# A graph network with feed-forward layers on one core: the dense layers taken block by block through the first gather pass, and the target one-hots of seven slots made by one instruction

## The chip, the cores and the metric

The kernel runs on one core of one Trainium2 chip. The metric is the device time of one execution in microseconds (us). Before the change it is 5313.63 us, the median of three runs (5313.40 to 5313.65).

## The reference

x is 6250 rows of 256 floats. There are 206250 edges (src, dst), sorted by dst, each with a type of 500. Four layers follow each other, each added to x:

```
x = x + L0_gnn(layernorm(x))     # feat: t1 = feat@W1; per edge t1[src] + (feat[src]*feat[dst])@W2, scaled by degrees,
                                 # summed over dst; leaky_relu(0.01); each row divided by its norm
x = x + L0_ffn(layernorm(x))     # x @ weight.T + bias
x = x + L1_gnn(layernorm(x))     # per edge: linear(h[src]*rel[type]) * sigmoid gate, normed by degrees,
                                 # summed over dst; then linear(h + sum)
x = x + L1_ffn(layernorm(x))     # for the 3124 rows with the highest score x@wr: gelu MLP, times the score
```

What matters here: both graph layers need, for every node, the sum over its incoming edges of a row that belongs to the edge's source. The second graph layer reads rows that depend on the first graph layer and on the dense layer behind it, of every node.

## The kernel before

The nodes are 49 blocks (NB) of 128 rows. X holds x in SBUF. A block's edges are padded to 35 slots (C) of 128 edges, so there are 1715 slots (SLOTS); seven slots (SG) are a step, five steps (SPB) a block. The table of rows (256 values and one extra column, padded to 260) is stored in DRAM, t1_d for the first layer and t2_d for the second.

A pass goes over all slots. GpSimd (POOL) issues one indirect gather per slot (`gathers`, L574) into `gath`, a ring of 18 slots (RG); a slot is free again when TensorE (PE) has used it, which it tells every sixth slot (MM, semaphore s_mm). `pick_edges` (L1221) lets VectorE (DVE) make a one-hot of the edges' targets, 128x128, for each slot: it compares iof, the numbers 0 to 127, with the column of dstf that belongs to the slot. `aggregate` (L702) multiplies one-hot and gathered rows on PE and sums a block's 35 slots in PSUM, bank 0 or 1 of psE; `block_out` (L950) lets ScalarE (ACT) copy a finished block to acc.

In the first pass the edges of each block are also sorted by type into quarters for the second pass: `marks`, `places` and `sends` (L1248 to L1297) on DVE, `rank` and `move` (L712, L723) on PE, copies with a scale (L967) and `places_out` (L955) on ACT. `in_place` (L1321 on) then turns the result into new srci, dstf and types, for all slots at once, after the pass.

Then come, each over all 49 blocks, the dense stage 0 (`dense`, L775 and L782, with `rows0`, `step0` on DVE and `squares` on ACT), which makes the first graph layer's output from the sums; the norms and the residual (L1452, L1456); the dense stage 1 (`rows1`, `step1`), the first feed-forward layer; the moments; and the table of the second pass (L1489), which SP stores in seven parts (`table`). Only then POOL starts the gathers of the second pass.

In the second pass DVE also multiplies the gathered rows with rows of the relation table, which PE picks into PSUM (`relations` L685, `products` L1240, two slots each), and makes further one-hots of the types (`one_hots` L1229). After it, messages and update, and the last feed-forward layer follow (from L1632 on).

Each engine works through its own instructions in order; between engines there are semaphores. `link` makes DVE wait for its own last instruction. `unordered` is a fallback for edge lists that don't fit the slots; on these inputs its branch isn't taken, but the register that decides it is loaded.

Of the kernel before, what the change touches and what calls it, by code (L numbers as in the profile page):

```python
# [7 lines left out]
F16 = mybir.dt.float16  # L8
# [112 lines left out]
def program(nc, x, src, dst, etype, w1_0, w2_0, b_0, wf, bf, rel, msg_w, msg_b, upd_w, upd_b,  # L121
            gate_w, gate_b, wr, br, w1, b1, w2, b2, out):
    ctx = ExitStack()
    with ctx:
# [8 lines left out]
        types_d = nc.dram_tensor("types_d", (SLOTS, P), F16).ap()  # L133
# [55 lines left out]
        o = 5 * W  # L189
        word = work[:, o:o + SLOTS].bitcast(I32)  # L190
        o += SLOTS
        typf = work[:, o:o + SLOTS]
        o += SLOTS
        types_h = work[:, o:o + TC * P // 2].bitcast(F16).rearrange("p (c e) -> p c e", e=P)
        early = work[:, o + TC * P // 2:o + TC * P // 2 + 3 * NB].rearrange("p (b c) -> p b c", c=3)
# [77 lines left out]
        inq = sb("inq", [P, NB])  # L273
        ssq = sb("ssq", [P, NB])
# [69 lines left out]
        s_st = sem("s_st")  # L344
        s_sc = sem("s_sc")
        s_cv = sem("s_cv")
        s_typ = sem("s_typ")
# [5 lines left out]
        s_typd = sem("s_typd")  # L353
# [9 lines left out]
        s_idx = sem("s_idx")  # L363
        s_trow = sem("s_trow")
# [5 lines left out]
        s_emb = sem("s_emb")  # L370
        s_ssq = sem("s_ssq")
# [81 lines left out]

        def blocks_of(r):
            return min(RB, NB - RB * r)

        @block.sync
        def _(sp):
# [25 lines left out]
            def table(layer, dram):  # L484

                for c in range(NB // 7):
                    sp.wait_ge(s_trow, layer * NB + 7 * (c + 1))
                    sp.dma_start(dram.rearrange("(b p) w -> p b w", p=P)[:, 7 * c:7 * c + 7, :],
                                 acc[:, 7 * c:7 * c + 7, :]).then_inc(s_td, 16)

# [7 lines left out]
            def unordered(layer):  # L498
                sp.load(any_drop, unsorted[0:1, layer:layer + 1])
                with sp.If_ne(any_drop, 0):  # L500
                    sp.wait_ge(s_uzero, layer + 1)
                    sp.dma_start(acc_d.rearrange("(b p) w -> p b w", p=P), acc[:, :, :]).then_inc(s_uacc, 16)
                    sp.wait_ge(s_uacc, 32 * layer + 16)
# [11 lines left out]
                    sp.dma_start(acc[:, :, :], acc_d.rearrange("(b p) w -> p b w", p=P)).then_inc(s_uacc, 16)  # L515
                    sp.wait_ge(s_uacc, 32 * layer + 32)

            any_drop = sp.alloc_register("any_drop_sp")
            table(0, t1_d)
            sp.wait_ge(s_typ, TC)  # L520
            full = (TC - 1) * P
            sp.dma_start(types_d[0:full, :].rearrange("(c p) e -> p c e", p=P), types_h[:, 0:TC - 1, :]).then_inc(s_typd, 16)
            sp.dma_start(types_d[full:SLOTS, :], types_h[0:SLOTS - full, TC - 1, :]).then_inc(s_typd, 16)
            sp.wait_ge(s_typd, 32)
            unordered(0)

            load_types(0)
            load_types(1)
            table(1, t2_d)
            for n in range(2, NB * SPB):  # L530
                load_types(n)
            unordered(1)
# [18 lines left out]
        def _(pool):  # L551
# [27 lines left out]
            def unordered(layer, table):  # L579
                pool.load(any_drop, unsorted[0:1, layer:layer + 1])  # L580
                with pool.If_ne(any_drop, 0):
                    with pool.Fori(0, UT // SK) as i:
                        for k in range(SK):
# [3 lines left out]
                            pool.wait_ge(s_td, 16 * (NB // 7) * (1 + layer))  # L587
# [8 lines left out]
                            pool.wait_ge(s_uacc, 32 * layer + 16)  # L596
# [4 lines left out]
                            pool.wait_ge(s_uacc, 32 * layer + 16)  # L601
                            pool.indirect_dma_start(acc_d, bass.IndirectOffsetOnAxis(ap=u_edge[:, 1:2], axis=0),
                                                    u_old, None).then_inc(s_uput[k], 16)

            pool.wait_ge(s_esrc, 16 * NB)
            pool.wait_ge(s_td, 16 * (NB // 7))
            gathers(0, t1_d)
            unordered(0, t1_d)
            pool.wait_ge(s_idx, 1)
            pool.wait_ge(s_td, 2 * 16 * (NB // 7))  # L610
            gathers(1, t2_d)
            unordered(1, t2_d)
# [30 lines left out]
        def _(pe):  # L643
            pe.sem_inc(s_st, 2)
# [84 lines left out]
            def first_pass():  # L729
                rank(0)  # L730
                for n in range(NB * SPB + 1):
# [6 lines left out]
                    if n > 0:  # L738
                        for k in range(SG):
                            move((n - 1) // SPB, SG * ((n - 1) % SPB) + k)  # L740
# [945 lines left out]
```

## Time and profile before

| | |
|---|---|
| median of 3 runs | 5313.63 us |
| profiled execution | 5320.06 us, its span 5318.3 us |
| PE busy | 3969.3 us (75%), mean granted clock 0.87 |
| DVE busy | 2844.8 us (53%) |
| ACT busy | 1348.0 us (25%) |
| POOL busy | 3385.6 us (64%) |
| DMA | 567.7 MB, 107 GB/s on average |

Times are in us unless marked ns. PE is TensorE's matmul, PEld its weight load, SP SyncE; L574 is line 574 of the kernel. A busy time counts neither semaphore nor branch instructions. The granted clock is the share of TensorE's full speed that the chip let through.

### The profile page before, as it was taken

What the parts mean: (1) busy time and instruction counts of PE and PEld (TensorE: products, weight loads), DVE (VectorE), ACT (ScalarE), POOL (GpSimd) and SP (SyncE); (2) the same over time, 40 slices, a digit from 0 to 9 for tenths busy, and PEclk for the clock granted to TensorE, in tenths of its full rate; (3) what the DMA queues carried; (4) which work ended last, traced back from release to release, by engine and by line L of the source; (5) the groups of instructions that cost most, each with busy time, mean ns of one, the idle gap of its engine ahead of it and who ended that gap; (6) DMA issues with size and microseconds to landing.
All of it is one profiled execution on the core that took longest, in us unless ns stands there. A gap on an engine that the chain in (4) does not pass through costs nothing.

```text
span 5318.3 us, 64872 instructions
## 1 busy us (share of the span) xinstructions
PE 3969.3 (75%) x19468; PEld 2668.9 (50%) x19468; DVE 2844.8 (53%) x10165; ACT 1348.0 (25%) x5769; POOL 3385.6 (64%) x3530
## 2 busy tenths in 40 slices
PE   6677777777777777778667777777777777778559
PEld 5533333333333333336445665555555565656448
DVE  8944445444454444447864444444444444445931
ACT  0055555555555555554200000000000000001212
POOL 0077777777777777771047777777777777774141
PEclk9977787777787777778889999999999999999879
DMA  4133333333333333331045555555555555553130
GB/s 105 51 105 106 106 106 106 106 107 106 107 107 106 107 106 106 107 106 36 0 132 133 131 132 132 132 131 132 132 131 132 132 132 132 133 131 96 39 111 21
DMA packets 263396, 567.72 MB, mean 107 GB/s; under 512 B 84810, under 2 KB 150439, under 8 KB 263086
## 3 DMA queue, kind: packets, MB, share of 16 engines
q0 software_dynamic: 168224, 466.63, 34.6%
q1 hardware_dynamic: 89438, 95.24, 5.8%
q8 instruction: 147, 2.41, 0.2%
q10 hardware_dynamic: 5424, 2.10, 0.2%
q14 instruction: 163, 1.34, 0.1%
HBM read 533.61 MB, written 30.12 MB: 106 GB/s over the span
## 4 chain that ended last, share of the span: by engine, by line
POOL 41%; issue 17%; PE 16%; DMA 16%; DVE 9%; DVEq 1%; ACT 0%; POOLq 0%; SPq 0%; ACTq 0%
POOL work L574 40%; DMA work<-t_d,srci 15%; PE psE L702 7%; PE psY L685 2%; DVE work L1164 2%; PE psY L659 1%; PE psY L898 1%; DVE work L1240 1%; PE psE L891 1%; PE psY L782 1%; PE psT L685 1%; DVE both L1108 1%; POOL accf L625 0%; PE psE L685 0%; DMA work<-in_dst 0%
## 5 line engine op out<-in xcount | busy, mean ns | idle before, releaser
L574 POOL DMA_INDIRECT work<-t_d,srci x3430 | 3278.2, 956 | 1583.8 <-issue 950.9
L702 PE MATMUL psE<-work,both 128*128 128x257 f32 x6860 | 2494.6, 478 | 1032.8 <-DMA work<-t_d,srci 522.2
L702 PEld LDWEIGHTS psE<-work,both 128*128 128x128 f32 x6860 | 1291.1, 221 | 1944.8 <-DMA work<-t_d,srci 1204.9
L967 ACT ACTIVATE work<-work 128x35 f16<-128x35 bf16 x5145 | 1127.3, 310 | 1043.2 <-DVE work L1293 1043.2
L1293 DVE TENSOR_SCALAR work<-iob,work 128x35 bf16<-128x35 bf16 x1715 | 278.0, 257 | 1091.1 <-PE psY L723 1072.7
L1221 DVE TENSOR_SCALAR both<-iof,dstf 128x128 f32<-128x128 f32 x3430 | 758.7, 307 | 19.6 <-PE psE L702 18.4
L950 ACT COPY accf<-psE 128x257 f32<-128x257 f32 x98 | 35.7, 364 | 2180.6 <-PE psE L702 2180.6
L1240 DVE TENSOR_TENSOR work<-work,psT 128x514 f32<-128x514 f32 x286 | 197.9, 692 | 376.4 <-DMA work<-t_d,srci 352.0
L1240 DVE TENSOR_TENSOR work<-work,psE 128x514 f32<-128x514 f32 (+1 forms) x286 | 197.5, 691 | 362.5 <-DMA work<-t_d,srci 349.9
L1240 DVE TENSOR_TENSOR work<-work,psY 128x514 f32<-128x514 f32 x286 | 197.8, 692 | 349.5 <-DMA work<-t_d,srci 332.4
L685 PE MATMUL psT<-relb,work 125*128 125x257 bf16 x2262 | 311.5, 282 | 21.5 <-DVE work L1229 21.5
L1297 DVE TENSOR_SCALAR work<-iob,work 128x128 f16<-128x128 bf16 x1715 | 327.0, 291 | 0.0
L685 PE MATMUL psY<-relb,work 125*128 125x257 bf16 x2253 | 310.4, 282 | 0.0
L685 PE MATMUL psE<-relb,work 125*128 125x257 bf16 x2247 | 306.9, 280 | 0.0
L685 PEld LDWEIGHTS psT<-relb,work 125*128 125x128 bf16 x2262 | 227.9, 101 | 95.4 <-issue 26.7
L685 PEld LDWEIGHTS psY<-relb,work 125*128 125x128 bf16 x2253 | 226.5, 101 | 72.4 <-issue 3.8
L685 PEld LDWEIGHTS psE<-relb,work 125*128 125x128 bf16 x2247 | 224.6, 100 | 71.2 <-issue 4.0
L723 PEld LDWEIGHTS psY<-work 128*128 128x128 f16 x1715 | 153.2, 130 | 67.4 <-issue 40.7
L659 PE MATMUL psY<-work 125*128 125x49 bf16 x1650 | 158.8, 269 | 19.1 <-DVE work L1164 18.6
L723 PE MATMUL psY<-work 128*128 128x105 f16 x1715 | 172.6, 263 | 0.0
L1164 DVE TENSOR_TENSOR work<-work,accf 125x3840 bf16<-125x3840 bf16 x110 | 162.3, 1537 | 2.1
L659 PEld LDWEIGHTS psY<-work 125*128 125x128 bf16 x1650 | 147.6, 143 | 30.3 <-DVE work L1164 30.3
(253 smaller groups left out, 2219.0 us busy)
## 6 DMA issues: line engine op xcount, KB each, us to landing
work<-t_d,srci POOLq DMA_INDIRECT x3430, 2.8
work<-types_d SPq DMA_DIRECT2D x245, 218.8 KB
t_d<-accf SPq DMA_DIRECT2D x14, 910.0 KB, 6.2
h_d<-accf SPq DMA_DIRECT2D x1, 6370.0 KB, 20.8
X<-in_x SPq DMA_DIRECT2D x1, 6144.0 KB
out<-X SPq DMA_DIRECT2D x6, 896.0 KB
work<-in_L_ffn_w SPq DMA_DIRECT2D x2, 1024.0 KB, 6.4
dstf<-in_dst SPq DMA_DIRECT2D x49, 17.5 KB, 1.7
```

The source lines that it names most:

```text
L574: pool.indirect_dma_start(gath[:, n % RG, :], None, table, bass.IndirectOffsetOnAxis(ap=srci[:, n:n + 1], axis=0)).then_inc(s_g[n % RG], 16)
L659: ins = nc.tensor.matmul(psY[:, 0, 0:NB], ohlo[:, n % 2, :, t], ohhi[:, n % 2, :, t], start=(n == t == 0), stop=(n == HN - 1 and t == HG - 1))
L685: ins = nc.tensor.matmul(rows, oht[0:RP, g % 2, at, :], relb[0:RP, part, c, 0:DW], start=((c, part) == (mine[0][0], 0)), stop=((c, part) = ...
L702: ins = nc.tensor.matmul(psE[:, b % 2, 0:DW], sel[:, third, k % SG, :], gath[:, n % RG, 0:DW], start=(k == 0), stop=(k == C - 1))
L723: ins = nc.tensor.matmul(psY[:, b % 2, 0:3 * C], to_q[:, n % 2, k % SG, :], to_s3[:, n % 2, k % SG, :, :].rearrange("p j s -> p (j s)"), s ...
L782: ins = nc.tensor.matmul(psY[:, par, 0:D], zts[:, par, t * P:t * P + P], weights(t), start=(t == 0), stop=(t == nk - 1))
L967: ins = nc.scalar.activation(to_s3[:, n % 2, i, j, :], to_s[:, n % 2, i, :], ACT.Copy, scale=load3[:, b // RB % 2, j, w:w + 1])
L1164: ins = v.tensor_tensor(one_hot[:, n % 2, :, :], bits[:, HG * n:HG * n + HG].unsqueeze(1).broadcast_to([NP, wide, HG]), counted[:, 0:wide, ...
L1221: ins = v.tensor_scalar(sel[:, n % 3, i, :], iof[:, :], dstf[:, k + i:k + i + 1], None, ALU.is_equal)
L1240: v.tensor_tensor(rows, rows, psR[q % 3][:, 0:many, 0:DW], ALU.mult).then_inc(s_po, 1)
L1293: ins = v.tensor_scalar(to_s[:, n % 2, i, :], iob[:, 0:C], spot_s[:, b // RB % 2, w + i:w + i + 1], None, ALU.is_equal)
L1297: ins = v.tensor_scalar(to_q[:, n % 2, i, :], iob[:, :], spot_q[:, b // RB % 2, w + i:w + i + 1], None, ALU.is_equal)
```

## The change

1. The dense work of the first two layers no longer runs between the passes. A block goes through it within the first pass, some steps after its last slot: `features` (step +5), `turn_features`, `messages` and `embeddings` (+5 to +7), `embed_norm`, `residual` (+8), `ffn_input`, `turn_ffn` (+9), `feed_forward` (+10), `fed` (+11), `table_row` (+12), and SP stores the block's row of the table (`store_row`). Sums are read from psE directly; `block_out` is no longer in the first pass. The bias of the feed-forward layer is added by a product with the identity.
2. `in_place` and the transposes of the types go by ranks of three blocks, within the pass.
3. A block's sum starts from a row loaded from acc_d (`load_old`), by a product with the identity. For this ACT writes zeros to acc_d ahead of the first pass, and `unordered` runs ahead of each pass.
4. `pick_edges` makes the seven one-hots of a step with one TENSOR_TENSOR of 128 x 896 instead of seven TENSOR_SCALAR of 128 x 128, in both passes.

The core of the diff:

```diff
             def pick_edges(layer, b, g):
...
-                for i in range(SG):
-                    ins = v.tensor_scalar(sel[:, n % 3, i, :], iof[:, :], dstf[:, k + i:k + i + 1], None, ALU.is_equal)
-                ins.then_inc(s_sel, 1)
+                v.tensor_tensor(sel[:, n % 3, :, :], iof[:, :].unsqueeze(1).broadcast_to([P, SG, P]),
+                                dstf[:, k:k + SG].unsqueeze(2).broadcast_to([P, SG, P]), ALU.is_equal).then_inc(s_sel, 1)
...
             def aggregate(layer, n):
                 b, k = n // C, n % C
-                if k == 0 and b >= 2:
-                    pe.wait_ge(s_ev, layer * NB + b - 1)
+                if k == 0:
+                    if b >= 2:
+                        pe.wait_ge(s_feat if layer == 0 else s_ev, b - 1)
+                    pe.wait_ge(s_old, 16 * (layer * NB + b + 1))
+                    nc.tensor.matmul(psE[:, b % 2, 0:DW], ident[:, :], old[:, 0:DW], start=True, stop=False)
...
+                    for m in due(n, 10):
+                        feed_forward(m)
+                    for m in due(n, 9):
+                        turn_ffn(m)
+                    for m in due(n, 6):
+                        messages(m)
+                    for m in due(n, 5):
+                        turn_features(m)
+                    for r in due3(n, 4):
+                        turn_types(r)
...
+            act.wait_ge(s_zero, 1)
+            act.dma_start(acc_d.rearrange("(b p) w -> p b w", p=P),
+                          zero.unsqueeze(1).broadcast_to([P, NB, W])).then_inc(s_zerod, 16)
             first_pass()
...
+                    for m in due(n, 12):
+                        table_row(m)
+                    for m in due(n, 11):
+                        fed(m)
+                    for m in due(n, 9):
+                        ffn_input(m)
+                    for m in due(n, 8):
+                        residual(m)
+                    for m in due(n, 7):
+                        embeddings(m)
+                    for m in due(n, 5):
+                        features(m)
+                    for r in due3(n, 3):
+                        in_place(r)
+
+            def features(b):
+                link(v.tensor_scalar(xhat, X[:, b, :], mean[:, b:b + 1], rstd[:, b:b + 1], ALU.subtract, ALU.mult))
+                dve.wait_ge(s_mm, summed(C * b + C))
+                if b >= 1:
+                    dve.wait_ge(s_feat_tp, b)
+                v.tensor_copy(inq[:, b:b + 1], psE[:, b % 2, D:DW])
+                v.tensor_scalar(has[:, b:b + 1], psE[:, b % 2, D:DW], 0.0, None, ALU.is_gt)
+                v.scalar_tensor_tensor(feat[:, 0:D], psE[:, b % 2, 0:D], degu[:, b:b + 1], xhat, ALU.mult, ALU.add)
+                v.scalar_tensor_tensor(feat[:, D:2 * D], psE[:, b % 2, 0:D], degu[:, b:b + 1], xhat,
+                                       ALU.mult, ALU.mult).then_inc(s_feat, 1)
...
+            def residual(b):
+                dve.wait_ge(s_norm, 2 * b + 2)
+                link(v.tensor_scalar(ssq[:, b:b + 1], ssq[:, b:b + 1], 1e-12, None, ALU.max))
+                link(v.reciprocal(ssq[:, b:b + 1], ssq[:, b:b + 1]))
+                link(v.scalar_tensor_tensor(X[:, b, :], embed[:, 1, :], ssq[:, b:b + 1], X[:, b, :], ALU.mult, ALU.add))
+                spread(b, 0).then_inc(s_var1, 1)
```

`due(n, j)` gives the block whose first step is j steps back, `due3` the same for ranks of three blocks.

## Rows read from the trace of the kernel before

**Rows 1.** Busy time by stretch: first pass, between, second pass, after it
```profile
core 0: us, PE busy (x) PEld busy (x) DVE busy (x) ACT busy (x) POOL busy (x), PEclk, DMA share, GB/s
266.28:2426.55 2160.27, 1622.08 (x5157) 827.81 (x5157) 1056.66 (x5606) 1144.28 (x5235) 1637.90 (x1715) 0.77 0.39 106
2426.55:2708.84 282.29, 190.15 (x934) 144.88 (x934) 243.64 (x657) 73.75 (x224) 0.95 (x2) 0.83 0.09 28
2708.84:4869.65 2160.81, 1679.15 (x10164) 1282.20 (x10164) 1060.63 (x2948) 18.03 (x48) 1638.40 (x1714) 0.96 0.53 131
```
**Rows 2.** Waits of POOL in the first pass: us, times, longest
```profile
POOL work L574 <- issue: 474.5, 1557, 0.3
POOL work L574 <- DMA t_d<-accf: 257.7, 1, 257.7
POOL work L574 <- PE psE L702: 47.8, 157, 0.3
```
**Rows 3.** Timeline: last gather, last sums copied, next gather (start, length)
```profile
2426.55 0.95 POOL L574 DMA_INDIRECT work<-t_d,srci  x1 [0.30 <-issue]
...
2430.63 0.38 ACT L950 COPY accf<-psE 128x257 f32<-128x257 f32 x1 [2.53 <-PE psE L702]
...
2708.84 0.94 POOL L574 DMA_INDIRECT work<-t_d,srci  x1 [281.34 <-DMA t_d<-accf]
```
**Rows 4.** Groups of instructions between the passes: count, busy us, mean ns
```profile
L775 PE MATMUL psT<-ident,both 128*128 128x128 f32 x294 | 53.0, 292 | 61.6 <-DVE both L1108 50.6 <-DVE both L1419 8.8
L782 PE MATMUL psY<-w1s,both 128*128 128x256 f32 x196 | 51.5, 386 | 0.0
...
L1000 ACT COPY both<-psT 128x512 f32<-128x512 f32 x49 | 28.7, 586 | 64.2 <-PE psT L775 64.2
...
L1418 DVE SCALAR_TENSOR_TENSOR both<-accf,degu,both 128x256 f32<-128x256 f32 x49 | 23.5, 479 | 0.9 <-issue 0.9
...
L1456 DVE BATCH_NORM_STATS2 st<-X x49 | 16.7, 412 | 1.0
```
**Rows 5.** DMA issues of the page: count, KB each, us to landing
```profile
t_d<-accf SPq DMA_DIRECT2D x14, 910.0 KB, 6.2
...
dstf<-in_dst SPq DMA_DIRECT2D x49, 17.5 KB, 1.7
```
**Rows 6.** While the first table is stored, columns as in rows 1
```profile
250.00:258.00 8.00, 0.00 (x0) 0.00 (x0) 8.00 (x26) 0.00 (x0) 0.00 (x0) 1.00 1.03 339
```
**Rows 7.** Group of L1277 in the first pass, columns as in rows 4
```profile
L1277 DVE TENSOR_TENSOR work<-work 128x420 f32<-128x420 f32 x16 | 9.6, 597 | 0.5
```
**Rows 8.** Timeline: one wide operation with two inputs in SBUF
```profile
22.07 5.89 DVE L1117 TENSOR_TENSOR accf<-ends,starts 125x5500 f32<-125x5500 f32 x1
```
**Rows 9.** Timeline at 397 us, DVE and POOL
```profile
397.27 0.60 DVE L1277 TENSOR_TENSOR work<-work 128x420 f32<-128x420 f32 x1
397.45 1.23 POOL L574 DMA_INDIRECT work<-t_d,srci  x1 [0.30 <-PE psE L702]
...
398.98 0.94 POOL L574 DMA_INDIRECT work<-t_d,srci  x1 [0.30 <-issue]
```
**Rows 10.** Timeline at 3008 us, DVE and POOL
```profile
3007.91 0.69 DVE L1240 TENSOR_TENSOR work<-work,psT 128x514 f32<-128x514 f32 x1 [0.70 <-DMA work<-t_d,srci]
3008.40 0.95 POOL L574 DMA_INDIRECT work<-t_d,srci  x1 [0.31 <-issue]
...
3009.65 0.95 POOL L574 DMA_INDIRECT work<-t_d,srci  x1 [0.30 <-issue]
```
**Rows 11.** Timeline: first and last full burst of one-hots in the second pass
```profile
2721.04 1.46 DVE L1221 TENSOR_SCALAR both<-iof,dstf 128x128 f32<-128x128 f32 x7
2721.35 0.99 POOL L574 DMA_INDIRECT work<-t_d,srci  x1 [0.30 <-issue]
...
4856.75 1.46 DVE L1221 TENSOR_SCALAR both<-iof,dstf 128x128 f32<-128x128 f32 x7
4857.11 0.95 POOL L574 DMA_INDIRECT work<-t_d,srci  x1 [0.30 <-issue]
```

More of the change, by code:

```diff
@@ L352, in program @@
         s_sqd = sem("s_sqd")
-        s_typd = sem("s_typd")
+        s_typd = [sem(f"s_typd{k}") for k in range(2)]
         s_oht = sem("s_oht")
@@ L452, in slots_of, with due, due3 @@
             return 2 * q, min(2, SLOTS - 2 * q)
+        def due(n, j):
+            b = (n - j) // SPB
+            return [b] if n >= j and (n - j) % SPB == 0 and b < NB else []
+        def due3(n, j):
+            return [r for r in range(RANKS) if n == SPB * (RB * r + blocks_of(r)) + j]
         def blocks_of(r):
@@ L730, in first_pass @@
                 rank(0)
-                for n in range(NB * SPB + 1):
+                for n in range(NB * SPB + SPB + 6):
                     b, g = n // SPB, n % SPB
@@ new lines, in first_pass, with features_turned @@
+                    if g == 2 and 0 < b <= NB:
+                        places_out(b - 1)
+                    for m in due(n, 11):
+                        deviation2(m)
+                    for m in due(n, 8):
+                        deviation1(m)
+                    for m in due(n, 7):
+                        embed_norm(m)
+            def features_turned(b):
+                act.wait_ge(s_feat_tp, b + 1)
+                if b >= 1:
+                    act.wait_ge(s_msg, b)
+                nc.scalar.copy(feat_t, psE[:, 2, 0:2 * D]).then_inc(s_feat_t, 1)
@@ L996, in dense @@
[L996 to L1015 removed]
+                    block_out(b)
@@ new lines, in fed, with table_row @@
+            def fed(b):
+                dve.wait_ge(s_fed, b + 1)
+                link(v.tensor_tensor(X[:, b, :], X[:, b, :], psE[:, 3, 0:D], ALU.add))
+                spread(b, 2).then_inc(s_var2, 1)
+            def table_row(b):
+                dve.wait_ge(s_std2, b + 1)
+                if b >= 2:
+                    dve.wait_ge(s_rowd[b % 2], 16 * (b // 2))
+                v.tensor_copy(mean[:, b:b + 1], mv[:, 2:3])
+                v.tensor_copy(row[:, b % 2, D:W], degu[:, b:b + 1].broadcast_to([P, W - D]))
+                link(v.reciprocal(rstd[:, b:b + 1], rstd[:, b:b + 1]))
+                link(v.tensor_tensor(rdeg[:, b:b + 1], rstd[:, b:b + 1], degu[:, b:b + 1], ALU.mult))
+                v.tensor_scalar(row[:, b % 2, 0:D], X[:, b, :], mean[:, b:b + 1], rdeg[:, b:b + 1],
+                                ALU.subtract, ALU.mult).then_inc(s_row, 1)
@@ L1381, in sweep @@
-            def sweep(stage, rows, step, after=None):
-                dve.wait_ge(s_ztp, stage * NB + 2)
-                rows(0, 0)
-                rows(1, 1)
-                settle()
-                if after:
-                    after()
-                    settle()
-                step(0, 0, first=True)
-                turns = (NB - 1) // G - 1
-                with dve.Fori(0, turns) as i:
-                    for k in range(G):
-                        step(1 + G * i + k, (1 + k) % 2)
-                for k in range(G):
-                    step(1 + G * turns + k, (1 + k) % 2, left=G - 1 - k)
@@ L1493, in _ @@
-            unordered(1)
+            dve.wait_ge(s_ev, NB)
             dve.sem_inc(s_acc, 1)
```

507 lines of the change are left out of this document (261 added, 246 removed).

## The prediction

> **What bounds the kernel now.** Read the four stretches first [rows 1]. GpSimd (POOL) issues 1715 gathers in each of two passes; each pass is 2160 us long, and together they hold 81% of the span. In both, POOL is busy for 1638 us, and that is all of them: a gather is busy for 0.95 us and the next starts 0.30 us later, so 1715 of them cost 1715 x 1.25 = 2150 us. POOL's waits in the first pass say the same [rows 2]: apart from the wait before the pass, its idle time is that 0.30 us of issue, and "PE psE" stands there for the same 0.3 us, not for a stall. TensorE idles a quarter of the first pass and has a granted clock of 0.77; VectorE is busy for 1057 us, ScalarE for 1144 us. So nothing but POOL's pitch sets a pass, and work put beside it is free as long as the pitch stays. Between the passes lies a stretch of 282 us in which POOL does two instructions [rows 1]: last gather of the first pass at 2426.55, first gather of the second at 2708.84 [rows 3]. That is the dense work of the first two layers. The sum is made against the profiled execution, 5320.1 us, which is 6.4 above the median of the runs; the last line subtracts this.
>
> **The seam.** The change moves the dense work into the first pass. What remains between the last gather and the next is the chain of the last block. The last sums arrive at 2430.6, 4.1 after the last gather started [rows 3]. Behind them come, one after the other, with durations of the same work in the stretch removed [rows 4]: two fused operations on psE with two small copies (1.3 us), four transposes (0.9), a copy of 512 columns (0.6), four products (2.1 at the speed shown, up to twice that), two more fused operations (0.9), a square and a root (1.0), the residual with its statistics (1.7), root, reciprocal and normalisation (1.0), in_place of the last rank with the pass over all of dstf (2.5), transposes, copy and products of the second layer (2.3), residual and statistics (1.3), root, scale and row (1.4), a store of 133 KB (2.4, between the 1.7 of 17.5 KB and the 6.2 of 910 KB [rows 5]). With the 4.1 that is 23.5; some fifteen crossings between engines and the load of the branch register on POOL add 2.5: 26 us in place of 282.3, so **minus 256** (minus 248 to minus 261).
>
> **The start.** ScalarE now writes zeros over acc_d, 6.5 MB, just before the table of 6.4 MB is stored. The transfer engines are full there already: 339 GB/s with a share of 1.03 [rows 6]. The zeros get a head start of some 4 us alone and have the rest to share; 13 MB at 339 GB/s is 38 us from about 240.5, so the table lands near 279 in place of 265, and the branch now ahead of the gathers costs one more: **plus 15** (0 if the queue of the table went first; 20, the 6.5 MB whole, if it went last). VectorE's marks and places start after the table instead of beside it; 12 us of them lie in front of slot 7 of PE, whose gather needs as long, and the ring of 18 slots covers the rest: nothing.
>
> **The one-hots.** Seven TENSOR_SCALAR of 128 columns, about 1.5 us a burst [rows 11], become one TENSOR_TENSOR of 896. Its length: 0.597 for 420 columns [rows 7] and 5.89 for 5500 [rows 8] give 1.04 ns a column, so 1.09 us. For VectorE that is a saving, and it is worth nothing, since VectorE doesn't set the pass. What counts is what it does to POOL. Look at 397 us [rows 9]: L1277 is a TENSOR_TENSOR with both inputs in SBUF. It is in flight when POOL's gather starts at 397.45; that gather takes 1.23 instead of 0.95, and the next comes 1.53 later instead of 1.25. L1277 ends at 397.87, 0.42 after the gather's start; the delay is 0.28. So POOL needs something 0.13 us into each gather and gets it when the VectorE instruction ends. Six of the sixteen L1277 fell so, each with a delay of 0.27 to 0.30; the ten that lay elsewhere in a gather cost nothing, nor did such instructions begun less than 0.17 us ahead of that point (the gather came first). The control is the product of the second pass, a TENSOR_TENSOR with one input in PSUM [rows 10]: 3007.91 to 3008.60 covers the point of the gather of 3008.40, and the pitch stays 1.25; so it is in 230 such coincidences, of which this one stands here, with a mean cost of 1 ns.
> The Trainium skill ("SBUF — State Buffer", section "Who interferes with whom") says that a VectorE instruction with two SBUF inputs contends with a GpSimd instruction that reads SBUF; the trace agrees, with 0.28 us. The same section infers that such an instruction leaves descriptor generation alone, as that only writes; by this the sum would be that of rival B.
>
> The new instruction holds the port from 0.17 to 1.09 us after its start, 0.92 of each 1.25. Each burst now meets one point. Where bursts fall evenly over the pitch, the mean delay is 0.92² / (2 x 1.254) = 0.34 us. First pass: the new steps between "sends" and the one-hots shift the phase differently in each of the five steps of a block, so I take the even value, 245 x 0.34 = **plus 82** (0 to 107, the latter with the 244 old phases put through this rule). Second pass: order and starts are unchanged, right behind a product, so the old phases hold. First burst: start 2721.04, end then 2722.13, POOL's point 2721.48, delay 0.65; last of 243: 4856.75, delay 0.60 [rows 11]. Over all 243 the mean is 0.54, **plus 131** (0 to 160). POOL has no slack that could take it: it waits for nothing in either pass. Given back: a pitch is 2160.3/1714 = 1.260 on average [rows 3], against 1.252 undisturbed, so 14 us a pass, much of it from the old bursts: **minus 15** for both (minus 28 to 0).
>
> **The dense work in the pass.** VectorE: some 25 instructions a block, about 8 us of each 46, less the 2.5 saved, on 49% busy. ScalarE: five short ones, 2 us of each 46, on 53%. Of VectorE's, two per block read two SBUF tensors (0.42 us; evenly spread 0.02 us of delay each) and three are wide scalar operations: **plus 5**. TensorE: it gets the seam's 190 us, 49 more products with the identity for the old sums and 49 for the bias, under 90 us. 1622 + 280 = 1900 of 2260 us, so covered, at today's clock. The waits: each stage of a block comes one step, 9 us, after the one before; the stall of VectorE for the block's last sums (up to 5 slots, 6 us) holds up only the next one-hots, which PE wants 2 slots later, and the ring of 18 slots stands between that and POOL. SP's load of the old rows and store of a row, 133 KB each, are small beside 106 GB/s. All at nothing; if the cover goes, rival C. At the end a branch less on the path: **minus 1**.
>
> **Sum**: 5320 - 256 + 15 + 82 + 131 - 15 + 5 - 1 = 5281, less 6.4: 5275 us, 0.7% faster.
>
> **Rivals.** B, no contention: the new instruction leaves POOL alone, as the products do. For it: they are TENSOR_TENSOR too. Against: they have one SBUF input, and L1277 with two delayed POOL each time it met the point. 5275 - 213 = 5062.
> D, the one-hots fall in the free quarter of the pitch in one of the passes: both are tied to a gather's landing, and a tied phase can be lucky. It would give 5275 - 82 - some of the 131, 5150 to 5190.
> C, slower: TensorE sets the first pass. Its work there in full-clock time is 1622 x 0.77 + 280 x 0.83 = 1480 us [rows 1]; with a pass of 2260 us it decides once the granted clock falls below 0.65. At 0.62 the pass would take 2390, so 5400. For it: the clock stood at 0.77 with TensorE a quarter idle. Against: the same engine with denser work in the second pass had 0.96, so more work should raise it.
> That the gain of the seam doesn't come would need the table rows to be late, and only the last block's are on the path.
>
> **How the numbers follow.** Main case 0.66, own range 5200 to 5345 (delays from 0.28 to 0.58 us a burst in place of the 0.43 of the sum); B 0.12; D 0.12; C 0.10. Leaving out B and the upper part of C gives 5130 to 5345. About 0.2%, 11 us, is what a measurement of this kernel can tell from no change. Faster (under 5303): 0.53 of the main case, B, D: 0.77. Same: 0.08. Slower: 0.06 of the main case and C, 0.15.
>
> **What would show it.** Seam between the passes' gathers near 26 us. First gather near 281. Passes of about 2230 and 2275 us; mean busy time of a gather up from 0.956 to about 1.02, with gathers of 1.2 to 1.9 us where a L1221-like TENSOR_TENSOR of 896 columns, of 1.09 us, lies over their start. TensorE waiting for gathers still. It would be wrong if the gathers keep a mean of 0.95 (B), or if POOL waits for PE for more than the 0.3 us of issue (C).

## The result and the profile after

The changed kernel takes 5263.19 us, the median of four runs (5257.03 to 5269.53), against 5313.51 us; the ratio is 0.9906, with a 95% interval of 0.9888 to 0.9923. The forecast was 5275 us. The profiled execution took 5257.0 us (span 5255.3) and that of before 5320.1. The profiled execution of the changed kernel is the fastest of its four runs, that of before was 6.4 us above its median, so the two profiles differ by 63 us and the medians by 50.

Busy time by stretch of the changed kernel: first pass, seam (the stretch from the last gather of the first pass to the first of the second), second pass. The columns are those of [rows 1].

```profile
core 0: us, PE busy (x) PEld busy (x) DVE busy (x) ACT busy (x) POOL busy (x), PEclk, DMA share, GB/s
279.86:2510.10 2230.24, 1681.33 (x6224) 1008.10 (x6224) 1255.05 (x5422) 1214.34 (x5537) 1708.12 (x1715) 0.82 0.41 109
2510.10:2537.45 27.35, 12.34 (x50) 8.51 (x50) 10.86 (x41) 4.72 (x20) 0.94 (x2) 0.68 0.09 27
2537.45:4806.64 2269.19, 1738.70 (x10276) 1308.37 (x10277) 967.59 (x1495) 17.97 (x48) 1747.09 (x1715) 0.95 0.53 128
```

The lengths in the second column give the whole change. The seam went from 282.3 us to 27.35: 254.9 gained. The first gather starts at 279.86 in place of 266.28: 13.6 lost. The passes are 70.0 and 108.4 us longer. Behind the last gather lie 449 us in both kernels. 254.9 - 13.6 - 70.0 - 108.4 = 62.9. VectorE's busy time in the second pass fell from 1061 to 968 us, and the pass grew all the same.

POOL's group in the first pass and in the second, and the new one-hots in each (count, busy us, mean ns, then idle time before them):

```profile
L642 POOL DMA_INDIRECT work<-t_d,srci x1715 | 1709.1, 997 | 793.4 <-issue 752.0 <-PE psE L785 41.4
...
L1317 DVE TENSOR_TENSOR both<-iof,dstf 128x896 f32<-128x896 f32 x245 | 265.4, 1083 | 22.8 <-DMA t_d<-accf 22.2
```
```profile
L642 POOL DMA_INDIRECT work<-t_d,srci x1715 | 1748.0, 1019 | 548.5 <-issue 522.9 <-PE psE L785 25.6
...
L1317 DVE TENSOR_TENSOR both<-iof,dstf 128x896 f32<-128x896 f32 x245 | 265.9, 1086 | 12.9 <-PE psE L785 12.9
```

A gather is busy for 0.997 and 1.019 us on average, in place of 0.956; 1715 x 0.041 = 70 and 1715 x 0.063 = 108 us. The growth of the passes is all in the gathers themselves, and none in POOL's waits. One of them, POOL's timeline and then VectorE's at 378 us:

```profile
377.54 0.95 POOL L642 DMA_INDIRECT work<-t_d,srci  x1 [0.30 <-PE psE L785]
378.80 1.74 POOL L642 DMA_INDIRECT work<-t_d,srci  x1 [0.31 <-issue]
380.83 0.94 POOL L642 DMA_INDIRECT work<-t_d,srci  x1 [0.30 <-issue]
```
```profile
378.24 0.48 DVE L1437 SCALAR_TENSOR_TENSOR accf<-psE,degu,accf 128x256 f32<-128x256 f32 x1
378.63 1.08 DVE L1317 TENSOR_TENSOR both<-iof,dstf 128x896 f32<-128x896 f32 x1
```

The one-hots end at 379.71. The gather's point, 0.13 us after its start, is 378.93; by the prediction's rule (a gather whose point falls into such an instruction, at least 0.17 us after the instruction's start, waits there until the instruction ends) the delay is 0.78 us, and the gather took 1.74 in place of 0.95. Put through all one-hots, the rule gives 77.7 us for the first pass and 113.3 for the second; the gathers that were hit (170 and 199 of them) were longer than an undisturbed 0.946 us by 78.3 and 114.1.

The seam in the timeline: last gather, the pass over dstf, the last row of the table, its store (the SP queue), and the next gather.

```profile
2510.10 0.95 POOL L642 DMA_INDIRECT work<-t_d,srci  x1 [0.30 <-issue]
...
2525.78 1.11 DVE L1512 TENSOR_SCALAR dstf<-dstf,gaps 128x1715 f32<-128x1715 f32 x1
...
2533.98 0.41 DVE L1481 TENSOR_SCALAR accf<-X,mean,rdeg 128x256 f32<-128x256 f32 x1
2534.42 0.32 SPq L542 DMA_DIRECT2D t_d<-accf  x1
...
2537.45 0.94 POOL L642 DMA_INDIRECT work<-t_d,srci  x1 [26.41 <-issue]
```

The start: the zeros and the table in the issues of DMA (us to landing at the end of the line), and the stretch in which both are in flight.

```profile
acc_d<-work ACTq DMA_DIRECT2D x1, 6370.0 KB, 31.3
t_d<-accf SPq DMA_DIRECT2D x7, 910.0 KB, 14.1
```
```profile
258.00:266.00 8.00, 0.00 (x0) 0.00 (x0) 0.00 (x0) 0.00 (x0) 0.00 (x0) 0.50 1.09 336
```

A part of the table takes 14.1 us to land in place of 6.2 [rows 5], at the same 336 GB/s as before [rows 6].

### The profile page after: what moved, and what is told of

It reads as the page before. It is cut to its first block, busy times and chain, and to the rows that moved or that the text cites. A ratio compares the mean times of both kernels' runs of the same rounds, so it can differ in the third digit from the quotient of the medians.

```text
span 5255.3 us, 62793 instructions
## 1 busy us (share of the span) xinstructions
PE 3909.4 (74%) x19765; PEld 2738.4 (52%) x19765; DVE 2711.5 (52%) x7884; ACT 1348.9 (26%) x5867; POOL 3564.5 (68%) x3530
## 4 chain that ended last, share of the span: by engine, by line
POOL 49%; issue 18%; PE 13%; DMA 13%; DVE 6%; DVEq 0%; SPq 0%; ACT 0%; POOLq 0%
POOL work L642 48%; DMA work<-t_d,srci 12%; PE psE L785 6%; DVE work L1261 2%; PE psY L988 1%; PE psE L981 1%; PE psY L765 1%; PE psY L739 1%; DVE work L1336 1%; PE psE L848 0%; POOL accf L706 0%; PE psT L765 0%; DMA work<-in_dst 0%; DVE both L1577 0%; DVE sqj L1590 0%
## 5 line engine op out<-in xcount | busy, mean ns | idle before, releaser
L642 POOL DMA_INDIRECT work<-t_d,srci x3430 | 3457.1, 1008 | 1341.9 <-issue 1274.9
L785 PE MATMUL psE<-work,both 128*128 128x257 f32 x6860 | 2314.7, 454 | 1075.5 <-DMA work<-t_d,srci 536.5
L785 PEld LDWEIGHTS psE<-work,both 128*128 128x128 f32 x6860 | 1265.0, 212 | 1861.8 <-DMA work<-t_d,srci 1068.5
L1038 ACT COPY accf<-psE 128x257 f32<-128x257 f32 x49 | 18.3, 374 | 2263.0 <-PE psE L785 2263.0
L1317 DVE TENSOR_TENSOR both<-iof,dstf 128x896 f32<-128x896 f32 x490 | 531.3, 1084 | 35.6 <-DMA t_d<-accf 22.2
L765 PE MATMUL psY<-relb,work 125*128 125x257 bf16 x2253 | 325.2, 291 | 0.0
L1261 DVE TENSOR_TENSOR work<-work,accf 125x3840 bf16<-125x3840 bf16 x110 | 163.2, 1538 | 1.1
## 6 DMA issues: line engine op xcount, KB each, us to landing
t_d<-accf SPq DMA_DIRECT2D x7, 910.0 KB, 14.1
```

What stands on the lines that cost most here:

```text
L642: pool.indirect_dma_start(gath[:, n % RG, :], None, table, bass.IndirectOffsetOnAxis(ap=srci[:, n:n + 1], axis=0)).then_inc(s_g[n % RG], 16)
L765: ins = nc.tensor.matmul(rows, oht[0:RP, g % 2, at, :], relb[0:RP, part, c, 0:DW], start=((c, part) == (mine[0][0], 0)), stop=((c, part) = ...
L785: ins = nc.tensor.matmul(psE[:, b % 2, 0:DW], sel[:, third, k % SG, :], gath[:, n % RG, 0:DW], start=False, stop=(k == C - 1))
L1261: ins = v.tensor_tensor(one_hot[:, n % 2, :, :], bits[:, HG * n:HG * n + HG].unsqueeze(1).broadcast_to([NP, wide, HG]), counted[:, 0:wide, ...
L1317: v.tensor_tensor(sel[:, n % 3, :, :], iof[:, :].unsqueeze(1).broadcast_to([P, SG, P]), dstf[:, k:k + SG].unsqueeze(2).broadcast_to([P, SG ...
```

## The experiments

The runs fell on two kinds of chips. On one chip the kernel before took 5314 us, as in its own runs; on four others, between 6056 and 6089 us. On those four TensorE, VectorE and ScalarE have gaps for which the trace shows no cause, here called stalls, and POOL waits beyond its 0.30 us of issue for 225 to 445 us a pass. "remote" in the lines from these chips is a wait that ended with a semaphore event whose instruction the profile doesn't show. Times are therefore compared only with those of the kernel before on the same chip; the busy time of a gather can be compared across them.

### One-hots back to seven instructions, and the zeros earlier

The zeros earlier, alone:

```diff
+            act.wait_ge(s_zero, 1)
+            act.dma_start(acc_d.rearrange("(b p) w -> p b w", p=P),
+                          zero.unsqueeze(1).broadcast_to([P, NB, W])).then_inc(s_zerod, 16)
             act.wait_ge(s_sq, 2)
             nc.scalar.activation(degu[:, :], degu[:, :], ACT.Sqrt).then_inc(s_sqd, 1)
...
-            act.wait_ge(s_zero, 1)
-            act.dma_start(acc_d.rearrange("(b p) w -> p b w", p=P),
-                          zero.unsqueeze(1).broadcast_to([P, NB, W])).then_inc(s_zerod, 16)
             first_pass()
```

> The changed kernel with ScalarE's write of zeros to acc_d issued some 190 us earlier, behind the sigmoid at about 46 us. Theory: the first table then has the transfer engines to itself, lands near 265 us, and the first gather starts near 266 in place of 279.9; about 5250 us, 13 to 14 less. Rival S (the early zeros hold up the loads of the edge windows, which are in flight from 48 us on, and with them the table): the first gather stays at 275 or later and the time at 5257 or above.

And with the old one-hots as well:

```diff
             def pick_edges(layer, b, g):
...
-                v.tensor_tensor(sel[:, n % 3, :, :], iof[:, :].unsqueeze(1).broadcast_to([P, SG, P]),
-                                dstf[:, k:k + SG].unsqueeze(2).broadcast_to([P, SG, P]), ALU.is_equal).then_inc(s_sel, 1)
+                for i in range(SG):
+                    ins = v.tensor_scalar(sel[:, n % 3, i, :], iof[:, :], dstf[:, k + i:k + i + 1], None, ALU.is_equal)
+                ins.then_inc(s_sel, 1)
```

> The changed kernel with seven TENSOR_SCALAR and with the early zeros. Theory: both gains add, as one shortens the passes and the other moves their start: first gather at 266, passes of 2160 us, seam of 27, 449 behind the last gather: about 5065 us. If the first pass is near TensorE's limit once POOL is free (rival P), it is 2180 or more and the total 5085 or more.

Measured on one chip, before at 5314.15: zeros earlier 5257.07 us (ratio 0.9895, 0.9880 to 0.9911); both 5065.55 us (0.9536, 0.9523 to 0.9549). The two differ by 191.5 us, and only the one-hots are different. Passes and seam of the two, first with the zeros alone:

```profile
265.82:2499.25 2233.43, 1685.77 (x6224) 1000.98 (x6224) 1255.98 (x5422) 1214.23 (x5535) 1711.11 (x1714) 0.82 0.41 109
2499.25:2525.31 26.06, 11.09 (x51) 7.30 (x50) 10.86 (x41) 5.13 (x22) 0.95 (x2) 0.74 0.09 28
2525.31:4806.41 2281.10, 1739.65 (x10277) 1303.43 (x10278) 967.00 (x1495) 18.01 (x48) 1758.75 (x1715) 0.96 0.52 128
```

then with both edits:

```profile
265.92:2427.39 2161.47, 1621.54 (x6224) 963.67 (x6224) 1349.94 (x6889) 1214.66 (x5536) 1639.10 (x1715) 0.85 0.42 112
2427.39:2453.43 26.04, 10.92 (x50) 7.30 (x50) 10.86 (x41) 4.77 (x20) 0.95 (x2) 0.78 0.09 28
2453.43:4612.44 2159.01, 1714.10 (x10279) 1310.94 (x10280) 1064.92 (x2965) 18.02 (x48) 1636.66 (x1715) 0.95 0.55 135
4612.44:5060.90 448.46, 314.88 (x1550) 263.27 (x1548) 243.46 (x649) 108.64 (x259) 100.35 (x83) 0.83 0.19 57
```

With seven instructions the passes are back at 2161 and 2159 us, and VectorE is busy for 94 and 98 us more in each. The dense work is still all in the first pass and adds 1.2 us to it. POOL's waits in that pass are as in [rows 2]:

```profile
POOL work L642 <- issue: 732.5, 1560, 257.4
...
POOL work L642 <- PE psE L785: 47.2, 155, 0.3
```

The "issue" holds the 257 us ahead of the first gather, and no wait for TensorE is longer than 0.3 us. VectorE has more to do than with the one instruction, and the passes are shorter all the same. So rival P falls here, and the new one-hots cost 191.5 us of the 255 that the seam gained. The expected 5065 us was met.

The zeros alone bring the first gather to 265.82, 14 us earlier, as expected, so rival S falls. The expected total, 5250, was missed by 7. The total fell by only 6 against the changed kernel measured elsewhere: the passes of this execution are 3.2 and 11.9 us longer than those of the changed kernel, with the same instructions in them. The rule gives 124.8 us for its second pass against 113.3: the phases between VectorE and POOL fall a little differently. The changed kernel's own four runs lie as far apart, 12 us; that the phases are the reason there is not shown.

### Undone alone, on a chip with stalls

The same edit of the one-hots, without the earlier zeros.

> The changed kernel with its one-hots again made by seven TENSOR_SCALAR; all of the dense work stays in the first pass. Theory (the one instruction with two SBUF inputs holds POOL up at the start of a gather): both passes go back to 2160 us from 2230 and 2269, gathers back to a mean busy time of 0.956, and the time to about 5080 us. Rival P (the passes are longer because TensorE or VectorE carry the dense work): the first pass stays at 2200 us or more, POOL waits for PE longer than the 0.3 us of issue, only the second pass could change; 5190 us.

Before took 6081.43 us on this chip, this kernel 5921.01 (0.9719, 0.9686 to 0.9753). The gathers of both passes are back at the old length, so that part of the theory holds:

```profile
L642 POOL DMA_INDIRECT work<-t_d,srci x1715 | 1634.4, 953 | 1240.9 <-issue 745.0 <-remote 307.8 <-PE psE L785 188.1
```

The absolute numbers of the expectation could not be met on this chip. Its passes are 2600 and 2536 us and POOL waits 188 us for TensorE in the first: on a chip like this, the dense work in the first pass is not free. The first pass of the kernel with PSUM one-hots below, which has no dense work, took 2482 on the same chip. That kernel differs in its one-hots too, so the 118 us are not all the dense work. The kernel before has the seven instructions and no dense work, but no trace from this chip; it took 17 us more than the PSUM one, which has the same second pass, so its first pass is by estimate some 2499 us, and about 100 us are left for the dense work. So the waits that rival P names are there on this chip, and absent where the stalls are.

### The one-hots alone, in the kernel before

```diff
             def pick_edges(layer, b, g):
...
-                for i in range(SG):
-                    ins = v.tensor_scalar(sel[:, n % 3, i, :], iof[:, :], dstf[:, k + i:k + i + 1], None, ALU.is_equal)
-                ins.then_inc(s_sel, 1)
+                v.tensor_tensor(sel[:, n % 3, :, :], iof[:, :].unsqueeze(1).broadcast_to([P, SG, P]),
+                                dstf[:, k:k + SG].unsqueeze(2).broadcast_to([P, SG, P]), ALU.is_equal).then_inc(s_sel, 1)
```

> The kernel before, with only its one-hots made by one TENSOR_TENSOR, in both passes; the dense work stays between the passes. Theory: first pass about 2255 us (244 bursts at their old phases, mean delay 0.44 us, less some 10 us of the old interference), second about 2270 as in the changed kernel; about 5515 us, 4% slower than before. Rival P: neither pass has dense work, so both stay at 2160 and the time at 5313.

> The kernel before with only its one-hots made by one TENSOR_TENSOR, in both passes, on another chip. In the earlier run of it the kernel before took 6081 us, and POOL waited for other engines for 235 and 287 us a pass, beside which the 110 us by which its gathers were longer could hide. Theory: where POOL waits for nothing, these come out in full: first pass about 2255 us, second about 2265, total about 5515 us. Rival T: the longer gathers are made up for by shorter waits here too; passes of 2160 to 2180, total 5315 to 5350.

> Once more the kernel before with only its one-hots made by one TENSOR_TENSOR, in both passes. On the two chips so far the kernel before took 6081 and 6056 us, with stalls of TensorE of 4 us and more, 750 us of them a pass, so POOL's longer gathers could hide behind them. Theory: on a chip where the kernel before takes 5314 us, the passes are about 2255 and 2265 us and the total about 5515. Rival T: 2160 to 2180 and 5315 to 5350. On a chip with those stalls: no change again.

All three fell on chips with stalls: 6065.04 against 6081.43 (0.9971, 0.9960 to 0.9982), 6048.61 against 6056.28 (0.9985, 0.9975 to 0.9995), 6069.09 against 6088.74 (0.9963, 0.9951 to 0.9975). The expected 4% did not show; the change of the one-hots alone was even a little faster. For a chip with stalls the last of the three expectations had said no change. Yet the gathers grew there too, with no dense work near them. First and second pass of the second of the runs:

```profile
L574 POOL DMA_INDIRECT work<-t_d,srci x1715 | 1736.7, 1013 | 1003.5 <-issue 486.7 <-DMA t_d<-accf 257.1 <-remote 225.7
```
```profile
L574 POOL DMA_INDIRECT work<-t_d,srci x1715 | 1726.3, 1007 | 1078.3 <-issue 505.2 <-DMA t_d<-accf 282.1 <-remote 260.8
...
POOL work L574 <- remote: 260.8, 118, 4.5
...
POOL work L574 <- PE psE L702: 30.3, 36, 6.4
```

A mean gather of 1.013 and 1.007 us, in the other two runs 1.011 and 1.010, 1.011 and 1.015. The rule, put through the phases of the six passes, gives 92.6 and 96.3, 99.5 and 93.8, 98.4 and 110.5 us; the hit gathers grew by 94.2 and 97.6, 100.4 and 94.5, 99.6 and 111.4. So the delays come from the new one-hots alone, without anything else of the change.

Where did the 190 us go? The passes of these kernels are 2482 to 2543 us long, 320 to 380 more than those of an undisturbed chip. Apart from what the gathers grew, that is time in which POOL waits beyond its 0.30 us of issue. In the second pass above, 261 + 30 us of it stand under "remote" and TensorE. The kernel of the next section, with seven instructions in its second pass on the same chip, has gathers of 957 ns there and these waits:

```profile
L574 POOL DMA_INDIRECT work<-t_d,srci x1715 | 1640.7, 957 | 1177.0 <-issue 525.8 <-DMA t_d<-accf 288.8 <-remote 280.7
...
POOL work L574 <- remote: 280.7, 109, 4.2
POOL work L574 <- PE psE L702: 81.7, 52, 5.6
```

Its second pass takes 2527.9 us against 2521.6. The gathers are 86 us shorter and the waits longer by 92: 71 of it under these two names (281 + 82 against 261 + 30), 21 under "issue" (525.8 against 505.2). So what the gathers lose is made up for by shorter waits. The reading is that a delay costs nothing where POOL would have waited for its slot anyway. This is rival T, and on these chips its forecast is right. On an undisturbed chip POOL has no such waits [rows 2]; there the pair of kernels above, 5257 and 5066 us, shows the price in time. The kernel before with only its one-hots changed was never measured on such a chip, and its expected time stays untested.

### One input of the one-hots in PSUM

The kernel before, with the first pass's one-hots as one TENSOR_TENSOR whose first input was copied into PSUM once, ahead of the pass. The second pass keeps its seven TENSOR_SCALAR in the first two runs, and takes the SBUF form in the third.

```diff
+            link(v.tensor_copy(psE[:, 3, 0:P], iof[:, :]))
...
             def pick_edges(layer, b, g):
...
+                if layer == 0:
+                    v.tensor_tensor(sel[:, n % 3, :, :], psE[:, 3, 0:P].unsqueeze(1).broadcast_to([P, SG, P]),
+                                    dstf[:, k:k + SG].unsqueeze(2).broadcast_to([P, SG, P]), ALU.is_equal).then_inc(s_sel, 1)
+                    return
                 for i in range(SG):
```

> The kernel before, with the one-hots of the first pass made by one TENSOR_TENSOR of 896 columns whose first input, the row of numbers, is read from a bank of psE that the first pass doesn't use; the second pass is as before. Theory: with one input in PSUM the instruction leaves POOL alone: first pass 2150 to 2160 us, mean busy time of its gathers 0.945 to 0.956, total about 5305 us. Rival R (what holds POOL up is any VectorE instruction of a microsecond): first pass about 2255 us, total about 5410.

> The kernel before with the one-hots of the first pass made by one TENSOR_TENSOR whose first input lies in PSUM, on another chip. In the earlier run its gathers of the first pass were 1 us longer in all than undisturbed ones. Theory: first pass 2145 to 2150 us, 10 or more less than with seven TENSOR_SCALAR, total about 5302 us. Rival R (any VectorE instruction of a microsecond holds POOL up): first pass 2255, total 5410.

> The kernel before with one TENSOR_TENSOR for the one-hots in both passes: its first input in PSUM in the first pass, in SBUF in the second. Theory: the gathers of the first pass keep a mean busy time of 0.946 to 0.948 us and those of the second go to 1.006 to 1.02; where POOL waits for nothing else, the first pass is 2145 to 2150 us, the second about 2265, the total about 5402. Rival R (any VectorE instruction of a microsecond holds POOL up): both passes 2255 to 2265, total 5515. Rival T (waits shrink as gathers grow): both 2160, total 5315.

All three fell on chips with stalls: 6064.67 against 6081.43 (0.9974, 0.9964 to 0.9984), 6047.50 against 6056.28 (0.9981, 0.9971 to 0.9991), 6054.20 against 6070.05 (0.9975, 0.9962 to 0.9988). The times tell nothing apart; the gathers do. The third run has both forms in one execution. Its first pass, input in PSUM, then its second, both inputs in SBUF:

```profile
L574 POOL DMA_INDIRECT work<-t_d,srci x1715 | 1628.9, 950 | 1108.0 <-issue 475.5 <-remote 351.7 <-DMA t_d<-accf 257.5
...
L1222 DVE TENSOR_TENSOR both<-psE,dstf 128x896 f32<-128x896 f32 x244 | 263.7, 1081 | 20.4 <-remote 14.9 <-DVE work L1288 1.7 <-issue 1.7
```
```profile
L574 POOL DMA_INDIRECT work<-t_d,srci x1715 | 1725.1, 1006 | 1085.9 <-issue 507.3 <-DMA t_d<-accf 285.0 <-remote 268.1
...
L1225 DVE TENSOR_TENSOR both<-iof,dstf 128x896 f32<-128x896 f32 x243 | 264.7, 1089 | 158.0 <-remote 86.5 <-PE psE L702 39.2 <-issue 31.8
```

The two forms are equally long, 1.081 and 1.089 us. With the input in PSUM a gather takes 0.950 us, the undisturbed length; with both in SBUF 1.006. In the first of the three runs the rule would give 61.9 us if both inputs lay in SBUF, and the gathers under the one-hots grew by -0.06. One such meeting in the third run, VectorE's timeline and then POOL's:

```profile
381.93 1.08 DVE L1222 TENSOR_TENSOR both<-psE,dstf 128x896 f32<-128x896 f32 x1
```
```profile
382.23 0.94 POOL L574 DMA_INDIRECT work<-t_d,srci  x1 [0.30 <-issue]
383.48 0.94 POOL L574 DMA_INDIRECT work<-t_d,srci  x1 [0.30 <-issue]
```

The gather's point is 382.36, and the one-hots cover it from 0.43 after their start to their end at 383.01. With SBUF inputs that would be 0.65 us of delay. So whether a VectorE instruction of this length holds POOL up is decided by where its inputs lie. Rival R, in which any VectorE instruction of a microsecond does, falls. A stall of these chips can be seen in the first of the runs; nothing that the trace shows released the gather of 483.70:

```profile
478.88 0.95 POOL L574 DMA_INDIRECT work<-t_d,srci  x1 [0.30 <-issue]
483.70 0.94 POOL L574 DMA_INDIRECT work<-t_d,srci  x1 [3.88 <-remote]
```

### The one-hots in two pieces

The changed kernel, with four and three slots in two instructions.

```diff
             def pick_edges(layer, b, g):
...
-                v.tensor_tensor(sel[:, n % 3, :, :], iof[:, :].unsqueeze(1).broadcast_to([P, SG, P]),
-                                dstf[:, k:k + SG].unsqueeze(2).broadcast_to([P, SG, P]), ALU.is_equal).then_inc(s_sel, 1)
+                for lo, hi in ((0, 4), (4, SG)):
+                    ins = v.tensor_tensor(sel[:, n % 3, lo:hi, :], iof[:, :].unsqueeze(1).broadcast_to([P, hi - lo, P]),
+                                          dstf[:, k + lo:k + hi].unsqueeze(2).broadcast_to([P, hi - lo, P]), ALU.is_equal)
+                ins.then_inc(s_sel, 1)
```

> The changed kernel with the one-hots of a step made by two TENSOR_TENSOR, four and three slots. Theory: what counts is how long the port is held in one piece; 0.52 and 0.39 us in place of 0.92 give, evenly spread, (0.52^2 + 0.39^2)/(2 x 1.254) = 0.17 us a step in place of 0.34, though VectorE is busy for longer (1.25 us in place of 1.09). First pass about 2195 us, second about 2215, total about 5165. Rival Q (the delay is in proportion to the time in which VectorE works with two SBUF inputs): passes as long as those of the changed kernel, 2230 and 2269, or some us longer; 5260 to 5275 us.

> The changed kernel with the one-hots of a step made by two TENSOR_TENSOR of four and three slots, on another chip. In the earlier run the gathers were 44 and 54 us longer than undisturbed ones in all, in place of 87 and 126. Theory: passes of 2188 and 2198 us, total about 5145 us. Rival Q (delay in proportion to VectorE's time with two SBUF inputs): 2230 and 2269, total 5260.

> Once more the changed kernel with the one-hots of a step made by two TENSOR_TENSOR, of four and three slots. In the runs before, on chips with stalls of TensorE, the gathers grew by 44 to 51 and 55 to 59 us a pass. Theory (square of the time held in one piece): on a chip without the stalls, passes of about 2200 and 2210 us, total 5165. Rival Q (in proportion to the time with two SBUF inputs): 2230 and 2269, total 5260.

5850.51 against 6081.43 (0.9616, 0.9600 to 0.9632), 5832.36 against 6056.28 (0.9630, 0.9611 to 0.9649), 5842.16 against 6070.05 (0.9627, 0.9606 to 0.9648), all on chips with stalls. First pass of the third run:

```profile
L642 POOL DMA_INDIRECT work<-t_d,srci x1715 | 1671.3, 975 | 1120.5 <-issue 745.4 <-remote 308.8 <-PE psE L785 66.2
...
L1318 DVE TENSOR_TENSOR both<-iof,dstf 128x512 f32<-128x512 f32 x243 | 166.6, 686 | 0.7 <-issue 0.2
L1318 DVE TENSOR_TENSOR both<-iof,dstf 128x384 f32<-128x384 f32 x244 | 134.6, 552 | 0.0
```

The pieces take 0.686 and 0.552 us, 1.24 together and so longer than the one of 1.08; yet the gathers grew by 35.2 and 40.7, 39.2 and 39.0, 35.3 and 39.4 us in the two passes of the three runs, in place of 78 and 114. The rule gives 33 to 37 and 38 to 40. For phases that fall evenly the delay goes with the square of the time held: 0.92² = 0.85 for the whole, 0.52² + 0.38² = 0.41 for the pieces, half. A cost that goes with the total time or the number of elements would have stayed or grown, so rival Q falls. The totals that were expected are for a chip without the stalls and stay untested.

The kernel with seven TENSOR_SCALAR, on the same chip as the first of these runs, took 5921.01, 70 us more than the split, though its gathers are the shorter ones (0.953 against 0.972 and 0.978). The loss lies in the first pass, 2600 against 2529 us; the second passes are 2536 and 2535. Why is open. One idea is that the stalls strike the instructions of an engine, so that fewer instructions meet fewer of them. The traces leave that open: VectorE's waits of over 1.5 us that end under "remote" are 143 with 6829 instructions in the first pass of the seven and 126 with 5633 in that of the pieces, but in the second pass 144 with 2964 and 147 with 1740.

## Why the prediction was right, and where it was not

**The bound.** Right. POOL's pitch set both passes before and after, and the growth of a pass is the growth of its gathers, 70 and 108 us.

**The seam.** Predicted 26 us left, minus 256; measured 27.35, minus 254.9. The chain added up in the prediction puts the end of the pass over dstf at 16.1 us after the last gather without the crossings; it ended at 2526.89, 16.8 after.

**The start.** Predicted plus 15, measured plus 13.6. The two stores shared one rate of 336 GB/s, and an earlier issue of the zeros took all of it back (first gather at 265.82).

**The one-hots, mechanism.** Right. A gather's point lies 0.13 us after its start, it is held there to the end of the VectorE instruction, and not at all with an input in PSUM. The rule worked out from sixteen L1277 gives every one of the seventeen passes with SBUF one-hots as one or two instructions to within some 6%. The section of the Trainium skill that the prediction weighed ("SBUF — State Buffer", "Who interferes with whom") names the two SBUF inputs as what contends, and the trace agrees, with 950 against 1006 ns above; its inference that descriptor generation is left alone does not hold for these gathers. The new instruction took 1.083 us, predicted 1.09. With the delays shown, rival B falls. Its 5062 us lies near the 5066 of the old one-hots with the zeros early, since the 15 us at the start, which B keeps, and the 15 given back, which it takes, cancel.

**The one-hots, size.** First pass: predicted plus 82, the even value of 0.34 us a burst; measured 78.3, 0.32. Second pass: predicted plus 131; measured 114.1, 0.46 a burst in place of 0.54. This is the step that failed: "order and starts are unchanged, so the old phases hold". The phases came out other than the old ones, and not even either (0.46 against 0.34). The reading is that a delayed gather moves all later gathers, and with them the one-hots that wait for what was gathered; no run isolates that. With the zeros issued earlier, which changes no instruction of the second pass, it was 125.7 or 0.51 a burst. So between two executions of the same instructions the phase moved by 0.05 us, and the old trace missed them by 0.08 and 0.03. That the even value came so near in the first pass is in part luck: the phases of the second were not even. Rival D, phases that fall in the free quarter, is not what happened: 170 and 199 of 245 bursts hit a gather.

**Given back.** Predicted minus 15 for the old bursts, both passes together. The hit gathers grew by 78.3 + 114.1 = 192.4 us and the passes by 178.4, so 14 us came back, whatever the dense work added included. With the seven instructions a gather takes 0.953 to 0.957 us, with the PSUM form 0.947 to 0.950, so the old bursts had that much to give. The term was right.

**The dense work in the pass.** Predicted plus 5; the pass of the version with early zeros and seven instructions is 1.2 us longer than before, and its second pass, with no dense work, 1.8 shorter, so nothing can be told from none. VectorE, ScalarE and TensorE had room for all of it. The cover was right for TensorE, and more so than predicted: its busy time was 1681 us in place of 1900, as its granted clock rose from 0.77 to 0.82 with the denser work. In full-clock time that is 1681 x 0.82 = 1379 us, where the prediction had 1480. Rival C falls where the chip has no stalls. (Its 5400 us starts from a pass of 2260; the prediction's own terms give 2240, and from there it is some 5425.) On chips with stalls POOL waits 188 us for TensorE in the first pass of the version with seven instructions, so the cover is thinner there.

**The sum.** The passes should have grown by 203 us and grew by 178. The rest of the sum is off by less than 2 us: seam 1.1, start -1.4, and the branch at the end, put at minus 1, gave nothing. So the profiled execution, 5257.0, lies 24 under the 5281 of the sum. The median lies 12 under the 5275: the subtraction of 6.4 took it that the profiled execution of the changed kernel would stand as high over its median as that of before; it stood 6.2 below. Two errors of opposite sign left the forecast nearer than its steps were; that is luck.

**What stays open.** What the stalls are. Why the split beats seven instructions there. And the times of the PSUM input and of the two pieces on an undisturbed chip: the gathers of the PSUM form let one estimate that with the zeros issued early it would come near the 5066 us of the seven instructions or a little below, but no run shows it, and the PSUM form was tried only in the first pass of the kernel before.

## What to carry to other kernels

Where one engine's pitch sets the time, look at each new instruction of the other engines for what it shares with that engine before counting what it saves: here VectorE got 90 us a pass back that nobody needed, and POOL paid 78 and 114 us for the second SBUF input. Keep such an operation in the scalar form, put one input in PSUM, or cut it in pieces; where the phases are spread, the delay goes with the sum of the squares of the pieces. On the chips with stalls the pieces were the fastest form of the changed kernel that was measured, so the choice is to be timed where the kernel will run. A change of two parts is to be taken apart: the seam was worth 255 us, and without the new one-hots, and with the zeros issued while the transfer engines were idle, the same kernel took 5065.55 us, 4.6% under before and the fastest version measured.

## What the runs showed of the hardware

TensorE's clock paid for its own extra work. Its busy time in the first pass was 1622 us before and 1621.5 in the version with early zeros and seven instructions, although the latter holds all the dense work (6224 records against 5157): the granted clock of the pass was 0.77 and 0.85. Where one-hots delay the gathers it was 0.82, with 1681 us.

The same program ran at two speeds on different chips, 5314 and 6056 to 6089 us, and the new one-hots, which cost 191 us in the changed kernel on the one, gained 0.15 to 0.4% in the kernel before on the other.

A VectorE instruction with two SBUF inputs that begins just ahead of a gather's point is itself the one that is longer. L1261 of the kernel before runs sixteen times on 128 x 105 elements. Six of them began 0.15 to 0.16 us ahead of a point and took 0.32 to 0.33 us; the other ten took 0.27. None of the six gathers was delayed. The first of the six, with its gather, whose point is 505.06:

```profile
504.90 0.33 DVE L1261 SCALAR_TENSOR_TENSOR work<-work 128x105 f32<-128x105 f32 x1
```
```profile
504.93 0.94 POOL L574 DMA_INDIRECT work<-t_d,srci  x1 [0.30 <-issue]
```
